# A Mamba-2 block and a mixture of experts on one core: narrower score tiles, one state scan a pair, residual and router keys on TensorE, new orders in the sequence stage

## What is computed

```python
proj = x @ W_in.T                      # xp, z, B, C, dt_low
dA = dtc * A; dAcs = jnp.cumsum(dA, axis=2)          # inside a chunk of 64
scores = einsum('bcihn,bcjhn->bcijh', Cc, Bc) * Lm * dtc[:, :, None]
y_intra = einsum('bcijh,bcjhp->bcihp', scores, xc)
chunk_state = einsum('bckhn,bckhp->bchnp', Bc, wx)
h = d * h + s                          # scan over the 32 chunks
y_cross = einsum('bcthn,bchnp,bcth->bcthp', Cc, h_states, exp(dAcs))
y = y_intra + y_cross + xp * D_param
y = y / rms(y) * norm_w * silu(z); attn = y @ W_out.T
x = layernorm(x + attn)
logits = -|x - keys|^2 + x @ rw.T + rb; top 4; softmax    # 16 experts
out = layernorm(x + sum_k w_k * (gelu(x @ w1[e_k].T + b1) @ w2[e_k].T + b2))
```

## Time and profile before

| what | us |
|---|---|
| device time, median of three | 387.39 |
| span of the profiled execution | 314.5 |
| TensorE busy in the span | 283.4 (90%) |
| VectorE busy | 204.3 (65%) |
| ScalarE busy | 209.2 (67%) |
| GpSimd busy | 143.7 (46%) |

### The profile page before, as it was taken

How to read it: one execution, slowest core, us unless ns; L and a number is a source line. 1 busy time by engine, 2 the same in 40 slices (tenths; PEclk the granted TensorE clock), 3 DMA queues, 4 the chain that set the end, 5 groups by cost and what they waited for, 6 DMA issues and landing times.

```text
span 314.5 us, 10587 instructions
## 1 busy us (share of the span) xinstructions
PE 283.4 (90%) x2948; PEld 250.6 (80%) x2949; DVE 204.3 (65%) x914; ACT 209.2 (67%) x725; POOL 143.7 (46%) x146
## 2 busy tenths in 40 slices
PE   2999899999999997899889899999999999997591
PEld 2986668687677775799779899999999999995480
DVE  2237768898888888866888566555655566641272
ACT  1475466575574743577667688888888889885064
POOL 1200000657456474777677775555555564424000
PEclk9979999999999999599999999999999999999697
DMA  6999920111111111342122232222222222100884
GB/s 212 300 336 374 415 95 2 40 39 57 38 58 48 39 58 47 87 103 78 48 83 90 80 92 72 65 81 71 67 69 67 70 68 60 42 12 6 305 273 92
DMA packets 25260, 33.30 MB, mean 106 GB/s; under 512 B 4299, under 2 KB 18020, under 8 KB 24832
## 3 DMA queue, kind: packets, MB, share of 16 engines
q1 hardware_dynamic: 20432, 23.30, 24.7%
q0 software_dynamic: 4352, 8.79, 7.9%
q10 hardware_dynamic: 432, 0.67, 0.7%
HBM read 21.76 MB, written 11.50 MB: 106 GB/s over the span
## 4 chain that ended last, share of the span: by engine, by line
PE 70%; DVE 11%; DMA 6%; issue 5%; ACT 5%; POOL 1%; DVEq 1%; POOLq 0%; ACTq 0%; SPq 0%
PE bank L774 16%; PE bank L752 15%; PE bank L747 4%; PE bank L539 4%; PE bank L553 4%; DMA yrows<-shared,idi 3%; PE bank L844 3%; PE bank L764 3%; PE bank L530 2%; PE bank L736 2%; PE bank L514 2%; PE bank L591 2%; DMA small<-in_small 2%; PE bank L601 2%; PE bank L563 2%
## 5 line engine op out<-in xcount | busy, mean ns | idle before, releaser
L1881 POOL DMA_INDIRECT yrows<-shared,idi x72 | 75.9, 1054 | 56.1 <-ACT shared L1790 32.6
L1860 POOL DMA_INDIRECT xrows<-rows_all,sli x64 | 62.4, 975 | 81.6 <-issue 63.4
L1769 ACT ACTIVATE shared<-bank,shared 128x128 f32<-128x128 f32 x256 | 73.2, 370 | 19.1 <-PE bank L752 19.1
L752 PE MATMUL bank<-shared 128*128 128x128 f32 x512 | 70.0, 281 | 2.5 <-issue 2.5
L774 PE MATMUL bank<-w2s,shared 128*128 x512 | 68.1, 276 | 0.8 <-DVE shared L1464 0.4
L752 PEld LDWEIGHTS bank<-shared 128*128 128x128 f32 x512 | 63.8, 196 | 3.9 <-issue 3.8
L774 PEld LDWEIGHTS bank<-w2s,shared 128*128 128x128 f32 x512 | 62.3, 192 | 1.4 <-issue 1.4
L1450 DVE COPY shared<-w1s 128x644 f32 x64 | 33.1, 517 | 28.5 <-issue 27.7
L1790 ACT ACTIVATE shared<-shared,idg 128x128 f32<-128x128 f32 x72 | 29.9, 418 | 7.1 <-DVE shared L1464 5.8
L1641 ACT ACTIVATE shared<-bank,small 128x256 f32<-128x256 f32 x64 | 25.1, 476 | 4.7 <-PE bank L539 4.7
L965 DVE TENSOR_TENSOR shared<-bank,small 128x512 f32<-128x512 f32 x32 | 21.2, 682 | 1.3 <-PE bank L553 1.3
(11 more groups left out here) (221 smaller groups left out, 472.0 us busy)
## 6 DMA issues: line engine op xcount, KB each, us to landing
shared<-xrows SPq DMA_DIRECT2D x64, 70.0 KB
w1s<-in_w1T SPq DMA_DIRECT2D x1, 4128.0 KB, 24.5
w2s<-in_w2T SPq DMA_DIRECT2D x1, 4096.0 KB, 22.9
w1s<-yrows SPq DMA_DIRECT2D x8, 512.0 KB, 7.9
yrows<-shared,idi POOLq DMA_INDIRECT x72
xrows<-zrow SPq DMA_DIRECT2D x1, 1120.0 KB, 13.9
xp_all<-in_xp SPq DMA_DIRECT2D x1, 1024.0 KB, 7.8
w1s<-in_b SPq DMA_DIRECT2D x1, 1024.0 KB, 20.9
```

Source lines behind the costliest of these rows:

```text
L752: m = mm(hidden_bank(u)[:, f * P:(f + 1) * P], w[:, f * P:(f + 1) * P], xbT[u][:, :], start=True, stop=True)
L1769: m = act(hT[u][:, f * P:(f + 1) * P], hidden_bank(u)[:, f * P:(f + 1) * P], ACT.Gelu, bias=w[:, F + f:F + f + 1])
L1860: po.indirect_dma_start(out=xrows, out_offset=bass.IndirectOffsetOnAxis(ap=sli[:, g, k:k + 1], axis=0), in_=rows_all[:, g, :], in_offset=N ...
L1881: po.indirect_dma_start(out=yrows, out_offset=bass.IndirectOffsetOnAxis(ap=idi[r][:, 0:1], axis=0), in_=yw[r][:, :], in_offset=None, bound ...
```

## The change

Six things change in the sequence stage, and both lists behind it are reordered.

1. `scores` become 16 products of 32x64 tiles with 128 columns, into four banks (3, 4, 6, 7); `block_diag` masks two heads instead of four, so two copies a tile.
2. `states` become eight products of 32x32 columns that write only the used blocks. `new_states` multiplies them once a pair, `carry` is one `tensor_tensor_scan` of 160 elements a pair, and ScalarE spreads the result (`states_out`, four copies over 32 partitions). The chunk factors are made on GpSimd ahead of its sends.
3. `project` makes only x (128 columns); B is turned from `cb` by two transposes, so `project(t)` needs `cb_copy(t)`.
4. `out_product` adds the residual by a product with `idkw`, and makes the router's logits in 16 more columns; `residual`, `x2_transpose`, `router` and the input `xp` are gone. `normed` moves to ScalarE (`rows_normed`), as does `pack_ids`; only pairs 6 and 7 keep the old way.
5. `y_cross` and `y_back` run once a pair, with the two tiles' products in turn; the skip products go to bank 5. `late` is now bank 1 alone.
6. `place`, `slots` and `gates` come one iteration later (s-3), `gated` too (s-2); a running `base` replaces the counts.

```diff
-                        for r in range(2):
-                            half = slice(r * Q, (r + 1) * Q)
-                            m = mm(bank[3 + r][q * Q:(q + 1) * Q, j * 256:(j + 1) * 256], c_[half, 2 + j, q * Q:(q + 1) * Q],
-                                   cbd[t % 2][half, j, q, :], start=True, stop=True, skip_group_check=True)
+                        for r, b in enumerate(score_banks):
+                            rows = slice(r * HR * NS, (r + 1) * HR * NS)
+                            m = mm(bank[b][q * Q:(q + 1) * Q, j * P:(j + 1) * P], c_[rows, 2 + j, q * Q:(q + 1) * Q],
+                                   cbd[t % 2][rows, j, q, :], start=True, stop=True, skip_group_check=True)
...
-                mm(bank[0][:, 0:384], xT_all[:, t * P:(t + 1) * P], winT[:, 0:384], start=True, stop=True
-                   ).then_inc(s1["pj_mm"], 1)
+                pe.wait_ge(s1["cb_act"], t + 1)
+                mm(bank[0][:, 0:D], xT_all[:, t * P:(t + 1) * P], winT[:, 0:D], start=True, stop=True)
...
+                for j in range(2):
+                    m = pe.transpose(bank[0][:, (j + 1) * P:(j + 2) * P], cb[t % 4][:, 2 + j, :], ident)
...
+                for q in range(NC):
+                    mm(late[:, q * DE:(q + 1) * DE], xTp[:, 2 * m_ + q, :], idkw[:, :], start=True, stop=False)
+                    m = mm(late[:, q * DE:(q + 1) * DE], yT[m_ % 2][:, q, :], woutn[:, :], start=False, stop=True)
...
+            def new_states(m_):
+                ve.wait_ge(s1["st_mm"], 2 * m_ + 2)
+                ve.wait_ge(gm_pool, 1 + (m_ >= 1) + (m_ >= NP // 2))
+                after(s1["e_act"], m_)
...
+            def carry(m_):
+                ve.wait_ge(s1["ds_dve"], m_ + 1)
+                at_m = hx[:, CP * m_:CP * m_ + 4 * HD * (CP + 1)]
+                ve.tensor_tensor_scan(at_m, gmx[:, m_, :], at_m, 0.0, ALU.mult, ALU.add).then_inc(s1["h_dve"], 1)
...
+            def states_out(m_):
+                if m_ == 0:
+                    ac.wait_ge(hs_set, 1)
+                ac.wait_ge(s1["h_dve"], m_ + 1)
+                after(s1["yc_mm"], m_ - 1)
+                for r in range(4):
+                    rows = slice(r * HR * NS, (r + 1) * HR * NS)
+                    m = act(hs[m_ % 2][rows, :, :, r * 2 * HD:(r + 1) * 2 * HD],
+                            chunk_states(m_)[rows, :, :, 0:CP].rearrange("p (j a) w c -> p c j (a w)", j=2), cp)
+                m.then_inc(s1["e_act"], 1)
```

More of the change, by code:

```diff
@@ L1234, in _ @@
             for s in range(1, NP):
-                tile(take_x, 2 * s, first=4)
-                tile(causal1, 2 * s - 1, first=3)
-                tile(causal0, 2 * s - 1, first=3)
-                pair(count_chosen, s - 3)
-                pair(residual, s - 2)
-                pair(res_stats, s - 2)
-                pair(res_moments, s - 2)
-                tile(scale1, 2 * s - 1)
-                pair(square_sums, s - 2)
-                pair(normed, s - 2)
-                tile(take_x, 2 * s + 1, first=3)
@@ L1246, in _ @@
-                tile(sum0, 2 * s, first=2)
-                tile(causal1, 2 * s, first=2)
-                tile(scale0, 2 * s, first=2)
-                pair(logits, s - 2)
-                tile(sum1, 2 * s, first=2)
+                pair(place, s - 3)
                 if s == EARLY + 2:
                     early_units()
-                tile(causal0, 2 * s, first=2)
+                pair(gated, s - 2)
                 if s == EARLY + 2:
                     early_shift()
-                pair(best, s - 2)
@@ L1267, in _ @@
                 if s == EARLY + 2:
                     early_place()
-                pair(chosen, s - 2)
-                pair(below_best, s - 2)
-                pair(pack_ids, s - 2)
-                tile(scale0, 2 * s + 1, first=3)
                 if s == EARLY + 2:
                     early_expert()
-                pair(y_scale, s - 1)
+                tile(causal0, 2 * s - 1)
                 if s == EARLY + 2:
                     early_start()
-                pair(y_add, s - 1)
+                pair(res_stats, s - 2)
@@ L1279, in _ @@
+                tile(take_x, 2 * s + 1, first=3)
+                pair(res_moments, s - 2)
+                pair(gates, s - 3)
+                tile(causal1, 2 * s)
+                pair(square_sums, s - 2)
+                pair(neg_means, s - 2)
+                pair(key_bias, s - 2)
                 if s == EARLY + 2:
                     early_rows()
-                pair(place, s - 2)
+                pair(logits, s - 2)
+                pair(best, s - 2)
                 if s == EARLY + 2:
@@ L1283, in _ @@
                     early_row()
-                pair(slots, s - 2)
+                pair(best_ids, s - 2)
+                pair(y_scale, s - 1)
+                pair(one_hot, s - 2)
+                pair(y_add, s - 1)
+                pair(chosen, s - 2)
+                tile(causal0, 2 * s)
+                if s < NP - 1:
+                    pair(new_states, s, first=1)
+                pair(below_best, s - 2)
                 if s == EARLY + 2:
                     early_diag()
-                pair(gated, s - 1)
@@ L1288, in _ @@
                 if s < NP - 1:
-                    tile(sum1, 2 * s + 1, first=3)
-                pair(gates, s - 2)
+                    pair(carry, s, first=1)
             links = [0]
@@ L1472, in moe @@
                 step3(Step(0, 4, b, True))
+            new_states(7)
+            carry(7)
+            place(5)
+            gates(5)
+            gated(6)
+            slots(5)
             causal0(15)
             causal1(15)
-            residual(6)
-            res_stats(6)
-            res_moments(6)
             early_table()
@@ L1557, in _ @@
             halves()
-            for b in range(18, NE - 1):
+            for b in range(18, 24):
                 moe(b)
```

629 lines of the change are left out of this document (318 added, 311 removed).

## The result

The changed kernel takes 393.61 us (median of four runs), the kernel before 386.41 us beside it. One of the four runs was disturbed (677.89 us, cause unknown) and the ratio leaves it out; the others are 391.29, 392.34 and 394.88. The ratio is 1.0148 with a 95% interval of 1.0095 to 1.0200: slower by 1.5%, where 379.4 us was forecast and 388 was the upper end. The profiled run took 392.34 us.

What follows compares the result with a forecast made beforehand. TensorE was taken to bound the 12.86 us iterations, with 72.9 us outside the span. Start 1.0, iteration 2 1.7 and iterations 3 to 6 6.2 gave 8.9 us, 8.0 after the bridge: 387.39 to 379.4 us, range 372 to 388.

Steps and rivals of the forecast that it cites:

- the first sentence: Whole kernel: 72.9 us lie around the 314.5 us span, untouched, so the span's change is added to 387.39.
- The sum: Whole kernel: start, loop and bridge together put pair 7's sends 8.0 us sooner, giving 379.4 us.
- loop of waits: Sequence stage iterations: the longest chain of waits between engines sets the new length, 11.3 us against 12.86.
- the prices: Sequence stage: costs per instruction group, saving TensorE 3.0 us an iteration, so it would need 9.3 us.
- a sign against the forecast: Sequence stage, ScalarE: `states_out` above 0.4 us a copy would show the forecast wrong.
- The start: Ahead of iteration 2: the change saves about 1.0 us by then.
- Clock: Rival, sequence stage: stalls lower TensorE's clock from 2.4 to 1.2 GHz, more than 400 us; 5%.
- Given back: Rival, bridge: iterations shorten but pair 7's sends do not follow, held up in GpSimd's chain, 384 to 387 us; 20%.
- the first give: Bridge, GpSimd: after 24 sends it comes at about 135.3 us; before 133 or after 138 would be wrong.
- Slower: Rival, sequence stage: ScalarE's queue sets the iteration at 14.0 us, total 394 us; 12%.
- Tight: Rival, sequence stage: the loop falls to GpSimd's pace of 10.1 us, total 374 us; 13%.

Runs made afterwards that it cites:

- a_copy: Changed kernel with a two-element GpSimd copy behind each send and each of the first 15 gives, on chip 0: 320.92 us, ratio 1.0152.
- a_late: Changed kernel with its 48 sends of pairs 0 to 5 held back until pair 4's gates are made, on chip 15: 392.03 us.
- a_again: Changed kernel, unchanged, run again on chip 15: 391.38 us.
- b_copy: Kernel before with a two-element GpSimd copy behind each send and each of the first 15 gives, on chip 0: 318.48 us, ratio 1.0095.
- x_direct: a_late plus eight extra plain transfers for each of pairs 0 to 3 at the sends' old place, on chip 9: 392.56 us.
- a_copy2: Changed kernel with a two-element GpSimd copy behind each send and each of the first 15 gives, on chip 5: 391.93 us.
- a_mid3: Changed kernel with a 512-column GpSimd memset behind each send and each of the first 15 gives, on chip 9: 352.21 us, ratio 0.8999.
- a_pow3: Changed kernel with a two-element GpSimd power behind each send and each of the first 15 gives, on chip 9: 372.57 us, ratio 0.9564.
- x_spaced: a_late plus eight extra unread indirect sends for each of pairs 0 to 3, a GpSimd power behind each, on chip 9: 389.22 us.

## Why the prediction was wrong

**The step that failed is the first sentence.** "72.9 us lie around it against the median of 387.39, and nothing in the change touches them": they lie inside, as stalls of TensorE beside dense sends, on chips 15, 9 and 5. Between the traced before and the one on chip 15, 36.7 us are lost by the `y_cross` of iteration 7 (143.91 against 107.18), 60.7 by the first send of pair 7 (216.92 against 156.19), and 73.1 by the end. The span of 314.5 answers to a chip like chip 0 (315.71 us in 13 runs). A trace and times of one kernel that differ by 19% do not describe one execution, and this was to be seen before forecasting. The sum then applied gains from a trace without stalls to times with them. The gains are real, but each iteration is there 10.1 us of sends and what comes behind them. In before that is TensorE's 12.3 us of work, less the part already done between the sends (10.7 of 10.8 us busy); in after it is the loop of waits, which less work on TensorE does not shorten (9.3 of 12.1 busy). Iterations 3 to 6 take 87.9 us in before and 87.7 in after on chip 15, where the forecast had after 6.2 us ahead. That the two sums are so near each other is in part luck: after is slower by 1.2 and 1.6 us in iterations 5 and 6, and faster by 1.7 and 1.4 in 3 and 4, where before's TensorE has the lower clock. The position in the iteration matters too: cut at its beginning (57.19 to 142.44 in after, 52.91 to 140.81 in before) the four are 2.7 us shorter in after.

**The loop of waits was right.** Forecast: 11.3 us an iteration against 12.86, TensorE busy for 9.1 to 9.6, scores 0.6 us, a wait of `y_intra` for `take_b` and a short one of the scores for VectorE. Without stalls on chip 0 (a_copy), five iterations, each from its first scores on, take 98.94 - 43.49 = 55.45 us, 11.1 each, against 64.12 in before:

```profile
98.94 0.70 PE L580 MATMUL bank<-shared 32*64 32x128 f32 x32 [0.15 <-DVE hx L941]
99.56 0.49 PE L552 MATMUL bank<-winT,xT_all 128*128 128x128 f32 x2
...
102.14 0.51 PE L660 MATMUL bank<-idkw,xTp 128*128 128x144 f32 x2
...
103.22 0.38 PE L552 MATMUL bank<-winT,xT_all 128*128 128x128 f32 x2
...
106.06 0.64 PE L621 MATMUL bank<-shared,xz 128*16 128x64 f32 x32 [1.35 <-ACT bs L1625]
106.63 0.69 PE L607 MATMUL bank<-hs,shared 128*64 128x64 f32 x16
107.21 0.69 PE L631 MATMUL bank<-cst,yiT 128*64 128x64 f32 x16
107.82 0.33 PE L593 MATMUL bank<-xz,bs 128*32 128x32 f32 x16
```

The line numbers are one higher than those of after. Scores take 0.62 us (98.94 to 99.56), `y_cross` 0.58 and `y_back` 0.61 (forecast 0.5 each), `out_product` 1.08 (1.0); the waits are 0.15 and 1.35 us. One slip stands in the prices: `states` at 0.64 less 0.29 us for each of two tiles is 0.7 saved, not 0.6. Two prices were too low: VectorE is busy for 8.6 us in an iteration, not 7.8, and a copy of `states_out` takes 0.43, not 0.29 (group of a_late, mean ns of one last):

```profile
L1603 ACT ACTIVATE hs<-hx 32x128 f32<-32x128 f32 x16 | 6.8, 428 | 0.1
```

That is over the 0.4 named as a sign against the forecast, and made ScalarE 8.6 to 8.9 us; the loop had room for it.

**The start was mis-sized, and it is where the change costs most.** Forecast: iteration 2 begins 1.0 us sooner than at 39.96. In a_copy it begins at 43.49, 3.5 us later, and in a_again at 46.23. It differs from run to run: in the 14 traces of the changed kernel and its variants iteration 2 begins at 41.4 to 47.1 us, in the six of before and its variants at 38.9 to 40.3, on chips with and without stalls. The same timeline and that of ScalarE, with the window of iteration 1:

```profile
29.71 0.68 PE L641 MATMUL bank<-wxd,xTp 128*128 128x128 f32 x4 [2.14 <-DVE woutn L878]
...
33.44 1.13 PE L565 MATMUL bank<-xT_all,winT 128*128 128x128 f32 x8 [1.79 <-issue]
...
38.32 1.06 PE L621 MATMUL bank<-shared,xz 128*16 128x64 f32 x32
39.30 1.12 PE L607 MATMUL bank<-hs,shared 128*64 128x64 f32 x16
```
```profile
30.70 1.77 ACT L1604 ACTIVATE hs<-hx 32x128 f32<-32x128 f32 x4 [1.96 <-DVE hx L948]
32.50 0.84 ACT L1618 ACTIVATE shared<-bank,small 128x256 f32<-128x256 f32 x2
```
```profile
30.32:43.49 13.17, 10.85 (x222) 8.81 (x221) 5.07 (x11) 6.44 (x19) 2.04 (x5) 0.74 0.67 286
```

TensorE's skip products wait 2.1 us for the router's constant that VectorE makes late. `states_out`, which I had costed only in the loop, stands ahead of the `block_diag` for which `project_cb` waits another 1.8. Behind these waits the granted clock is at its half level (1.2 GHz) from 34.9 to 41.8 us. How the 3.5 us divide between these three was not tested. The start is the rival "Clock" in small: `y_intra` takes 0.98 us there from start to start (38.32 to 39.30) and 0.57 at full clock (106.06 to 106.63).

**"Given back" came true on chip 0, at the sends of pair 7.** Its 20% were too low there. On chip 0 the first product of the experts comes at 123.5 us in a_copy and at 128.0 in b_copy, but pair 7 is sent from 156.43 and 157.24. GpSimd in a_copy:

```profile
107.00 0.96 POOL L1865 DMA_INDIRECT xrows<-rows_all,sli  x1 [0.94 <-DVE rows_all L1102]
...
141.09 1.03 POOL L1915 DMA_INDIRECT yrows<-shared,idi  x1 [0.18 <-issue]
...
151.43 0.98 POOL L1915 DMA_INDIRECT yrows<-shared,idi  x1 [1.28 <-issue]
152.56 1.69 POOL L1929 TENSOR_TENSOR ge<-cst,gd 128x8 f32<-128x8 f32 x1
156.43 1.03 POOL L1865 DMA_INDIRECT xrows<-rows_all,sli  x1 [2.18 <-DVE sli L1091]
```

Iteration 7 begins at 98.94 and not at 95.2 (start 4.5 us worse, loop 0.8 better than the forecast), and pair 4 is sent 8.1 us into it as forecast, from 107.0. From there to the first give, at 141.09 where 135.3 was forecast (and 138 was named as the latest), GpSimd never waits for more than 0.7 us: 3.7 of these 5.8 us are the late iteration 7, and most of the rest are the copies behind 24 sends. Seven gives and `last_gates` take 13.2 us where 11.2 were forecast (two waits, 0.95 and 1.28), and then the slots of pair 7 are 2.2 us late, the mechanism named in that rival. Of a gain of 4.5 us 0.8 is left, and the median of a_copy, with the 10.6 us a pair that the copies make, is even 2.4 us above that of b_copy (their profiled runs are as long as each other, with spans of 315.6 and 315.8; the other three of a_copy take 320.46 to 322.18). So without stalls the change looks worth nothing, or a small loss: 0.8% with the copies, 1.9% with the powers (364.01 against 357.23). But after itself was never run on such a chip beside before: that stays open, and so does where these 2.4 us are.

**The other rivals.** "Slower" had the right sign and the wrong engine: ScalarE never set the iteration. "Tight" did not come: 11.1 us is the loop of waits, not GpSimd's pace. "Clock" came in part (0.69 in an iteration with sends), but as a result of the stalls, which it adds to; without sends the loop has 1.00.

**What stays open** is the mechanism by which indirect transfers hold up TensorE, and what differs between the chips. GpSimd's sends have the same length in both (0.96 us, every 1.26), so its side shows nothing. The Trainium skill says in "Trainium Architecture — The Big Picture", "What this means for kernel authors", that the engines' side of SBUF and the side of the DMA can't contend. The iteration of 11.0 us beside plain transfers (x_direct) agrees with it. The 2.1 to 2.8 us for a matmul beside indirect ones (a_late) have a cause that no run here shows; it need not be SBUF. The Trainium skill's "NOTIFIC — the notification-queue block", "7.1 Overflow: three behaviours, one of which stalls the engine", says that in one of its settings a full queue of trace records holds up its producer; no run here shows or excludes that.

## What to carry over

Put the span of a profile beside the time of its own run before a sum is made: where they differ by more than a few microseconds, the trace is of another kind of execution, and the difference is a cost that is still to be found, not a constant to carry along. Where an engine is stalled from outside, price a change by what comes behind the stall: less work on the engine that is held up wins nothing if a chain of waits is as long as before. Price the start too, wait by wait, and not only the loop: here it took back half of what the loop gave on chip 0, and more than all of it on chip 15. If TensorE's results are late beside a row of indirect transfers, try 0.7 us or more of other work between two of them, and measure on each chip: it gave 10% on chip 9, and 0.96 us of it cost 13 to 15% on chip 0.

## What the hardware showed

- The same kernel took 315.7 us on chip 0 and 387 to 391 us on chips 15, 9 and 5, each run within 2% of the median on its chip.
- On the latter, indirect transfers 0.30 us apart slow TensorE to one matmul in 2.1 to 2.8 us (a_late), and each costs 1.3 to 1.5 us (40 in 50.4 us; two of them 3.1); 0.37 us apart they are no better (a_copy2). 0.70 us apart, eight cost about 3 us together (a_mid3); 0.96 us apart, about 1 (a_pow3, x_spaced).
- Plain transfers from the same queue, eight in 4.3 us, cost nothing that shows (x_direct, 11.0 us).
- A matmul's recorded start can be 8.8 us ahead of the start of the engine that waits for its result (89.97 and 98.74 in after).
